# A transformer block on one NeuronCore: the opening's blocks on the whole array in another order, a norm moved to GpSimd, and a shorter patience in the last half

## The reference

```python
x = x + layernorm(attention(layernorm(x)))
x = x + layernorm(ffn(layernorm(x)))

def attention(x):          # w_q, w_k, w_v, w_o: 256 x 256
    q, k, v = (x @ w.T split into 16 heads of 16)
    weights = softmax(q . k * 0.25)          # over 1024 keys
    return concat(weights . v) @ w_o.T

def ffn(x):                # W_r, W_k, W_v: 256 x 256, mu_r, mu_k: 256
    x_prev = x shifted by one token (zeros first)
    r = sigmoid((mu_r * x + (1 - mu_r) * x_prev) @ W_r.T)
    k = (mu_k * x + (1 - mu_k) * x_prev) @ W_k.T
    return r * (relu(k) ** 2 @ W_v.T)
```

## Time and profile before

| | before |
|---|---|
| median of 3 runs | 1284.59 us (1283.14 to 1287.94) |
| the profiled execution | 1282.99 us, span 1281.2 us |
| TensorE matmul busy | 1258.9 us, 98% |
| ScalarE busy | 1064.4 us, 83% |
| VectorE busy | 786.1 us, 61% |
| GpSimd busy | 269.5 us, 21% |
| DMA | 112.72 MB, mean 88 GB/s |

### The profile page before, as it was taken

One profiled execution on the slowest core, in us unless ns is written; L12 is line 12 of the kernel. 1 busy time (PEld: TensorE's weight loads), 2 busy tenths in 40 slices (PEclk: granted clock), 3 DMA queues, 4 the chain that ended last, 5 costly groups with the idle time before them and its releaser, 6 DMA issues.

```text
span 1281.2 us, 25644 instructions
## 1 busy us (share of the span) xinstructions
PE 1258.9 (98%) x10684; PEld 606.2 (47%) x10684; DVE 786.1 (61%) x1736; ACT 1064.4 (83%) x1153; POOL 269.5 (21%) x351
## 2 busy tenths in 40 slices
PE   8999999999999999999999999999999999999997
PEld 5544444444444444444544444444444445534345
DVE  6653746748465773847567584666747466463747
ACT  3688888888888888888888888888888888898962
POOL 1000112222211321212221221223222122222211
PEclk9999999999999999999999999999999999999999
DMA  4365563316612185124933166321761129300001
GB/s 152 97 148 167 100 130 83 100 51 127 118 54 83 51 176 106 34 67 102 146 84 91 45 110 131 72 84 51 152 113 49 36 78 171 84 1 30 5 1 34
DMA packets 61798, 112.72 MB, mean 88 GB/s; under 512 B 6512, under 2 KB 31344, under 8 KB 61616
## 3 DMA queue, kind: packets, MB, share of 16 engines
q1 hardware_dynamic: 61360, 109.60, 37.7%
q10 hardware_dynamic: 288, 1.05, 0.3%
HBM read 68.42 MB, written 41.94 MB: 86 GB/s over the span
## 4 chain that ended last, share of the span: by engine, by line
PE 90%; DVE 6%; ACT 2%; issue 1%; POOL 1%; DMA 1%; ACTq 0%; DVEq 0%
PE O L603 37%; PE S L584 25%; PE M L350 14%; PE M L337 11%; PE M L247 2%; ACT PT L591 2%; DVE sth L700 1%; DVE A L709 1%; PE M L487 1%; DMA A<-w_dram 1%; DVE mvh L702 0%; POOL rsh L705 0%; DVE xnT L413 0%; DVE xB L735 0%; DVE xnT L375 0%
## 5 line engine op out<-in xcount | busy, mean ns | idle before, releaser
L591 ACT ACTIVATE PT<-S 128x1024 f32<-128x1024 f32 x1024 | 1003.5, 1025 | 162.2 <-PE S L584 161.8
L603 PE MATMUL O<-PT,V 128*17 128x512 f32 x4096 | 538.9, 598 | 0.0
L584 PE MATMUL S<-QS,KS 50*128 50x512 f32 x2048 | 464.6, 450 | 3.9 <-ACT PT L591 3.9
L584 PEld LDWEIGHTS S<-QS,KS 50*128 50x128 f32 x2048 | 211.1, 183 | 452.5 <-ACT PT L591 373.2
L603 PEld LDWEIGHTS O<-PT,V 128*17 128x17 f32 x4096 | 67.8, 95 | 139.7 <-issue 137.9
L704 POOL TENSOR_SCALAR veh<-mvh 128x2 f32<-128x2 f32 x96 | 22.4, 233 | 495.9 <-DVE mvh L702 494.2
L913 DVE SCALAR_TENSOR_TENSOR A<-Z,M 128x512 f32<-128x512 f32 x30 | 20.4, 681 | 160.5 <-PE M L350 160.5
L337 PE MATMUL M<-xnT,WH 64*128 64x512 f32 x512 | 112.3, 395 | 3.2 <-DVE xnT L413 3.2
L350 PE MATMUL M<-WH,cT 64*128 64x256 f32 (+1 forms) x496 | 83.2, 281 | 2.8 <-DVE rec L660 2.8
L350 PE MATMUL M<-WH,xnT 64*128 64x256 f32 x512 | 84.7, 278 | 0.3 <-DVE xnT L413 0.3
L350 PE MATMUL M<-WH,B 64*128 64x256 f32 (+1 forms) x496 | 81.5, 278 | 0.0
(11 more groups left out here) (129 smaller groups left out, 1617.0 us busy)
## 6 DMA issues: line engine op xcount, KB each, us to landing
scr<-p SPq DMA_DIRECT2D x124, 256.0 KB
QS<-scr SPq DMA_DIRECT2D x56, 256.0 KB, 6.0
KS<-scr SPq DMA_DIRECT2D x56, 256.0 KB, 11.0
QS<-scr SPq DMA_DIRECT2D x70, 128.0 KB, 5.8
KS<-scr SPq DMA_DIRECT2D x68, 128.0 KB, 8.0
xA<-x_dram SPq DMA_DIRECT2D x16, 512.0 KB, 7.4
xB<-x_dram SPq DMA_DIRECT2D x16, 512.0 KB, 5.2
out_dram<-xB SPq DMA_DIRECT2D x15, 512.0 KB, 3.0
```

What stands on the lines that cost most here:

```text
L584: fn = lambda e, p=p, a=a, rows=rows: e.matmul(PS[p][:, a, :], KS[qd][rows, p, kt * 128:kt * 128 + 128], QS[qd][rows, p, hf * 512:hf * 512 ...
L591: e_fn = lambda e, p=p: e.activation(PT[i % 2][:, 2 * p:2 * p + 2, :], PS[p][:, :, :], ACT.Exp, scale=SCALE)
L603: fn = lambda e, j=j: e.matmul(PO[32 * j:32 * j + 17, :], V[b % 2][:, kt, 4 * qd + j, :], PT[i % 2][:, j, :], start=(kt == 0), stop=(kt == 7))
```

## The change

The opening's blocks are emitted one at a time by a new function `alone` (all 128 rows in one go, the way the end of the kernel already did it), in another order, and four of ten warming matmuls go. Statistics of both halves of the first batch are taken together, the second half's norm goes to GpSimd. The loop begins when V0 is there; V1, Q00 and K00 run alone within its first two steps, with ScalarE still as copier. The direct blocks' copies are all on ScalarE. The first quad's rows get their own counter, though the scores wait for both. The statistics and the norm of the second batch, and the first spread, move by steps. In EVEN, K00 stands ahead of T10. In the last half unit the longer patience (`age` 2) ends at step 5 and not 20, and the last heads' resting work is put first.

```diff
-            rows_all = sp.dma(... s_rows, *lines)
+            tok = sp.dma(... s_rows if qd else s_rows0, *lines)
+            rows_of_quad[min(qd, 1)] = tok
...
-        def ln1_norm(b, g):
+        def ln1_norm(b, g, eng=dve):
             for t in range(4 * g, 4 * g + 4):
-                d = dve.op(lambda e, t=t: e.tensor_scalar(xA[:, t, :], xA[:, t, :], mv[:, t, 0:1],
+                d = eng.op(lambda e, t=t: e.tensor_scalar(xA[:, t, :], xA[:, t, :], mv[:, t, 0:1],
                                                           rs1[:, t:t + 1], ALU.subtract, ALU.mult), ln1_r[g])
...
-                    if n:
-                        h = dve.op(lambda e, rows=rows: e.tensor_copy(dst[rows, p, cols], m[rows, :]), tok)
-                    else:
-                        h = act.op(lambda e, rows=rows: e.activation(dst[rows, p, cols], m[rows, :], ACT.Copy), tok)
+                    h = act.op(lambda e, rows=rows: e.activation(dst[rows, p, cols], m[rows, :], ACT.Copy), tok)
...
-                waits = [rows_all, *here[b, qd, 0, hf], *here[b, qd, 1, kt // 4]]
+                if b == qd == hf == 0:
+                    waits = [*rows_of_quad, flagged, here[0, 0, 0, hf][p], here[0, 0, 1, kt // 4][p]]
+                else:
+                    waits = [*rows_of_quad, *here[b, qd, 0, hf], *here[b, qd, 1, kt // 4]]
...
             if kt == 7:
                 until_rest(quad(g, qd))
+                if i == len(steps) - 1:
+                    resting.insert(0, resting.pop())
...
-        FIRST = "Q00 K00 V2 K01 V3 Q10 K10 K11 Q01 Q11"
-        EVEN = "W3 T00 T01 y0 y1 Q00 T10 K00 T11 z0 z1 k0 k1 r0 r1 v0 v1 Q01 K01"
+        ALONE = ("V1 Q00", "K00")
+        FIRST = "V2 K01 V3 Q10 K10 K11 Q01 Q11"
+        EVEN = "W3 T00 T01 y0 y1 Q00 K00 T10 T11 z0 z1 k0 k1 r0 r1 v0 v1 Q01 K01"
...
-        FIRST_SPREADS = {3: [(1, (0, 1), (0,))], 6: ...
+        FIRST_SPREADS = {2: [(1, (0, 1), (0,))], 6: ...
...
+        def alone(b, u, word, then=None):
+            block(b, u, word)
+            waiting[-1].seen = step_now[0]
+            piece = choose(0)
+            if isinstance(piece, Turn):
+                turn(piece)
+                return
+            m = PM[piece.bank[0]]
+            ops = piece.half(m, 2)
+            for k, (_, fn) in enumerate(ops):
+                if k + 1 < len(ops):
+                    pe.quiet(fn, *(piece.waits[0] if k == 0 else ()))
+                else:
+                    p = pe.op(fn)
+            if then:
+                then()
+            until_rest(piece.done(piece.bank[0], m, p))
...
         keep_warm(2)
         ln1_stats(0, 0)
+        ln1_stats(0, 1)
         ln1_norm(0, 0)
+        ln1_norm(0, 1, pool)
...
-        run("T00 T01")
-        keep_warm(2)
-        ln1_stats(0, 1)
+        for word in ("T00", "T01"):
+            alone(0, 0, word)
+        keep_warm(1)
...
-        meanwhile[:] = [lambda: ln1_norm(0, 1), lambda: (split_weights(["wv"]), sum_heads(), keep_warm(1)),
-                       lambda: (keep_warm(2), sum_all()), lambda: None, lambda: split_weights(["wq", "wk"])]
-        run("D00 E00 D10 E10 T10 T11 V0 V1 E01 E11")
+        alone(0, 0, "D00")
+        alone(0, 0, "E00", sum_heads)
+        alone(0, 0, "T10")
+        alone(0, 0, "D10", sum_all)
+        alone(0, 0, "T11")
+        split_weights(["wv"])
+        alone(0, 0, "E10")
         flagged, = flagging
+        alone(0, 0, "E01")
+        alone(0, 0, "E11")
         load_xa(1)
         scores(0, 0, 1)
-        copier[0] = "dve"
+        alone(0, 0, "V0")
+        split_weights(["wq", "wk"])
...
-            if u == 0:
-                for word in FIRST.split():
-                    block(0, -1, word)
-            for word in (EVEN, ODD)[hf].split():
-                block(b + 1, u - 1, word)
             for s in range(32):
                 i = step_now[0] = 32 * u + s
+                if (u, s) == (0, len(ALONE)):
+                    copier[0] = "dve"
+                    for word in FIRST.split():
+                        block(0, -1, word)
+                if s == (0 if u else len(ALONE)):
+                    for word in (EVEN, ODD)[hf].split():
+                        block(b + 1, u - 1, word)
...
-                age = 2 if b + 1 == B and s < 20 else 1
+                if u == 0 and s < len(ALONE):
+                    for word in ALONE[s].split():
+                        alone(0, -1, word)
+
+                age = 2 if b + 1 == B and s < (5 if hf else 20) else 1
...
-                if u == 0 and s in (2, 3, 4, 5):
-                    (ln1_stats, ln1_norm)[s % 2](1, s // 2 - 1)
+                if u == 0 and s in (4, 5, 6, 7):
+                    (ln1_stats, ln1_norm)[s % 2](1, s // 2 - 2)
```

More of the change, by code:

```diff
@@ L118, in sandwich_kernel @@
         s_first = [[sem(f"s_first{i}"), 0] for i in range(10)]
-        s_rows, s_wide = [sem("s_rows"), 0], [sem("s_wide"), 0]
+        s_rows, s_rows0, s_wide = [sem("s_rows"), 0], [sem("s_rows0"), 0], [sem("s_wide"), 0]
         s_scr = [[sem(f"s_scr{i}"), 0] for i in range(3)]
@@ L159, in sandwich_kernel @@
         load_weights(sp, T[0], "wr")
+        rows_of_quad = [None, None]
         for qd, i, a in itertools.product(range(4), range(2), range(2)):
-            rows_all = sp.dma(lambda e, a=a, i=i, dst=(KS, QS)[i][qd]: e.dma_start(
+            tok = sp.dma(lambda e, a=a, i=i, dst=(KS, QS)[i][qd]: e.dma_start(
                 dst[64 * a + SHIFT:64 * a + SHIFT + 2, :, :].bitcast(F32).rearrange("s p n -> s (p n)"),
-                PT[i][0:2, :, :].rearrange("s j n -> s (j n)")), s_rows, *lines)
+                PT[i][0:2, :, :].rearrange("s j n -> s (j n)")), s_rows if qd else s_rows0, *lines)
+            rows_of_quad[min(qd, 1)] = tok
+        rows_all = rows_of_quad[1]
         on_set = dve.op(lambda e: e.memset(On[:, :], 1.0))
@@ L455, in done @@
                 v_ready[b, g] = d
-                if meanwhile:
-                    meanwhile.pop(0)()
                 state["qk_read"] = p
@@ L490, in p_direct @@
             return Block("ahead", half, xnt_of(0, n, "wide"), done, tokens=n)
-        meanwhile = []
         def spread(b, qd, tensors=(0, 1), halves=(0, 1), counter=None):
@@ L523, in on_pe @@
             def on_pe(e):
-                for w_ in exps + all_here + [rows_all]:
+                for w_ in exps + all_here + rows_of_quad:
                     e.wait_ge(w_[0], w_[1])
@@ L560, in on_sp @@
                 e.wait_ge(g_dve, 19 * n + 19)
-                e.wait_ge(rows_all[0], rows_all[1])
+                for w_ in rows_of_quad:
+                    e.wait_ge(w_[0], w_[1])
                 for a, p, t in itertools.product(range(2), range(2), range(2)):
@@ L949, in sandwich_kernel @@
         SPREAD_AT = (12, 18, 26)
-        FIRST_SPREADS = {3: [(1, (0, 1), (0,))], 6: [(1, (1,), (1,))], 7: [(2, (0, 1), (0,))], 8: [(2, (1,), (1,))],
+        FIRST_SPREADS = {2: [(1, (0, 1), (0,))], 6: [(1, (1,), (1,))], 7: [(2, (0, 1), (0,))], 8: [(2, (1,), (1,))],
                          10: [(3, (0, 1), (0,)), (3, (1,), (1,))], 16: [(qd, (0,), (1,)) for qd in range(4)]}
@@ L1105, in sandwich_kernel @@
                 rest_no_more()
[L1106 to L1119, removed]
+            alone(B, 2 * B - 1, word)
         rest_no_more()
```

## The result

The changed kernel takes 1274.80 us in the median (1273.65 to 1275.03, 4 executions), the one before 1285.07 beside it: a ratio of 0.9912, 95% interval 0.9897 to 0.9928. It is faster, by 0.9%; the forecast of 1278.2 was 3.4 too high. The profiled executions, 1282.99 and 1274.69, lie 8.3 apart, less than the medians do; what the record shows of the difference stands with the ninth experiment.

What follows compares the result with a forecast made beforehand. TensorE was taken to set the pace in the middle, so only the ends could win: 3.65 + 2.7 = 6.35 off the profiled 1282.99 is 1276.6, or 1278.2 off the median 1284.59; range 1273 to 1283.

Steps and rivals of the forecast that it cites:

- the two terms that were forecast: Gains at the kernel's two ends: 3.65 us at its start and 2.7 behind the loop, 6.35 in sum.
- the forecast's own sign: Long middle of the kernel: it stays as before; the forecast is wrong if the middle has changed.
- The opening: Start of the kernel: third step's values end at 42.3 and not 45.95, a gain of 3.65 us.
- the 0.6 for VectorE's wait: Start: VectorE's second wide-weights subtraction waits for one GpSimd norm instruction, making D00 0.6 us later.
- a sign of being wrong: Start: the forecast is wrong if the low clock appears in new gaps of 0.5 to 1.6 us.
- The step that failed: Loop's EVEN order: K00 ahead of T10 issues the same instructions and DMAs, costed at nothing.
- The end: Behind the loop: later work comes 2.4 us earlier, the clock stays up; 2.7 taken, bounds 1 to 4.
- the loop's own delay: Last half unit: two more longer steps (0.6) and a stall at k0 (0.8 to 1.2), 1.4 to 1.9 us later.
- a constant 1.6: Whole kernel: the profiled execution of before lies 1.6 us below the median, so 1276.6 becomes a median of 1278.2.
- the first: Start: the first exponential's 6.6 us stay whole; 1275.3, or 1274 with no lateness of D00; chance 0.2.
- the second: End: stalls at k0 and z0 or v0 cancel the age change, opening gives 2; 1281 to 1284; chance 0.28 including middle.
- the third: Start: slow GpSimd norms delay T10 and the first scores; gain gone at about 2.4 each, 1291 at 4; chance 0.04.

Runs made afterwards that it cites:

- the ninth experiment: The kernel before, with five warming matmuls at the very start and not three: 1284.39 us, ratio 0.9990 against the kernel before.
- the third experiment: The changed kernel with the old EVEN order and the old end, so the opening alone: 1280.80 us, ratio 0.9953 against the kernel before.
- the seventh experiment: The changed kernel with k's mixing ahead of the heads' transposes in step 16 of the last half unit: 1273.51 us, ratio 0.9901 against before.

## Why the prediction was right, and where not

The direction and the range were right; one step was missed, and one median was taken for another. There was luck in it: in the profile the two terms that were forecast, 6.35, came to 4.4, and 3.9 that was put at nothing made up for it. By the forecast's own sign, that the middle has changed, its account is wrong there.

**The opening** came out as forecast with the clock up, 3.65 and 3.75 in the third experiment, but by two errors that cancel. D00 began at 14.48 there and not 15.35: GpSimd's norms were sized at 0.6 each and take 1.2 (the first 1.95), and the 0.6 for VectorE's wait did not come. And from Q00's start to the third values it was 9.6 and not 8.8; half of this is the blocks alone, put at 1.4 to 1.5, where Q00 takes 1.67 and K00 1.59. In between, from D00 to Q00, the chain was right: 18.1 against 18.15. (Its 19.65 for D00's VectorE part is 0.3 more than its own terms, 16.75, 1.21 and 1.40, give.) The changed kernel's profile reached D00 at 15.55, near the forecast's 15.35, for a reason that was not in the forecast, the low clock at the Gram products. That low clock was named as a sign of being wrong, but it came in a gap that the old opening has too. The warning of the Trainium skill, GPSIMD Engine Reference, section 4.1, against elementwise work on GpSimd did not hold here: the slower engine was free until T10 needed the norm, and it ended at 17.75, 0.8 ahead of that. Its best case of section 3.1, an estimate of 0.4 here, was far from the 1.21 measured. The lock that SBUF — State Buffer, section Who interferes with whom, describes was seen from the other side: GpSimd's first norm, begun while VectorE's subtractions ran, took 1.95, the next three 1.21 to 1.22.

**The step that failed** is the sentence that K00 ahead of T10 issues the same instructions and costs nothing. The instructions are the same; the bank that K00 gets is not. The order was worth 3.92 in the profile and 4.4 by itself, the largest part of the change there. The stall stood in the page of before, 3.2 us of TensorE in a kernel whose pace TensorE sets.

**The end** was sized at 2.7 and gave 1.7 in the profile. The mechanism was right: v1's last stage and v0's norm inside the loop, the transposes within 2 us of the last values, no fall of the clock behind them, k0 late by 1.2 for GpSimd's operand, which the seventh experiment took away. The term that was mis-sized is the loop's own delay, 1.4 to 1.9 in the forecast and 2.63 measured: z0 in step 13 waits too, and its step takes 2.95 where 2.24 is normal.

**The median.** The forecast put the profiled sum on the median by a constant 1.6. The sum was 1.9 short (1276.6 for a profiled execution that took 1274.69). The other 1.5 of the miss is the constant: the changed kernel's profiled execution lies 0.1 below its median and not 1.6. The 1.6 was no constant but the low clock in most executions of before (35 of 46), of which the ninth experiment's profile shows one, worth 3.1; the changed kernel's four executions lie within 1.4 of each other. Where the clock was low in the others stays open.

Of the rivals, the first had a time of 1274 to 1275.3, and that is where the kernel landed, but by chance and not by its mechanism: of 6.3 us at the first exponential 2.7 remained. Of the second the stalls came, at k0 and at z0, but not its sum; the third did not happen.

## What to carry to other kernels

In a kernel bound by one engine, read every row in which that engine waited, however small its share: 0.5 us in each of six places was worth more than the whole new opening in the profile. An order of blocks is also an order of buffers, so moving a block asks which buffer it now gets and whose work that buffer still waits for. A single profile shows one draw of the clock; compare medians, and the mean clock of each execution, before trusting a difference of 2 us.

## What the runs showed of the hardware that was not expected

- A GpSimd scalar operation with two operands per partition on 128x256 float32 takes 1.21 us (the second to fourth norm of the changed kernel), as long as its product on twice the elements, 128x512 (1.15); VectorE needs 0.41 for it.
- A GpSimd instruction that began at 12.19, while VectorE's two subtractions ran to 13.02, took 1.95 and not 1.21, as if it had waited for both; VectorE lost nothing (1.28 against 1.29).
- TensorE's clock fell to the lower level behind stretches with 0.69 of 2 us busy at the start, and with 1.11 of 2 at the first steps in the ninth run; the same instructions ran at the higher level in other executions. At the start the difference lay in when the clock first rose: the same warming matmuls took 4.25 us in the execution with the fall and 5.06 in the profile of before.
